# Keys and queries of self-attention moved one group of heads at a time, first maxima between expert sums, and a new order of the stages with warm-up matmuls and early table loads

## The reference, cut to what matters

```python
# layer 0, per sequence
weights = softmax(q @ k.T); evidence = weights @ v
combined = concat([nx, evidence, anchor])
router_probs = softmax(combined @ router_W + router_b)
h = silu(combined @ e_w1 + e_b1); expert_out = h @ e_w2 + e_b2
routed = sum(expert_out * router_probs)
x = x + sigmoid(silu(combined @ gate_w1 + gate_b1) @ gate_w2 + gate_b2) * (routed @ out_w + out_b)
# layer 1, per sequence
h = layernorm(x) * (1 + scale_msa) + shift_msa
x = x + (mha(q, k, v) @ self_o_w + self_o_b) * gate_msa       # self-attention, 512 x 512 scores a head
h = layernorm(x) * norm2_g + norm2_b
x = x + mha(h @ q_w + q_b, context k, context v) @ cross_o_w + cross_o_b
h = layernorm(x) * (1 + scale_mlp) + shift_mlp
x = x + (gelu(h @ mlp_w1 + mlp_b1) @ mlp_w2 + mlp_b2) * gate_mlp
```

## Time and profile before

| | us |
|---|---|
| Median of three runs | 295.75 (294.68 to 296.03) |
| The profiled execution's own time | 295.85 |
| Its span in the profile | 294.1 |
| PE busy | 247.7 (84% of the span) |
| DVE busy | 170.0 (58%) |
| ACT busy | 148.3 (50%) |
| POOL busy | 45.5 (15%) |
| Mean granted clock of TensorE | 0.918 |

### The profile page before, as it was taken

One profiled execution on the slowest core, in us unless ns is written; L12 is line 12 of the kernel. 1 busy time (PEld: TensorE's weight loads), 2 busy tenths in 40 slices (PEclk: granted clock), 3 DMA queues, 4 the chain that ended last, 5 costly groups with the idle time before them and its releaser, 6 DMA issues.

```text
span 294.1 us, 4801 instructions
## 1 busy us (share of the span) xinstructions
PE 247.7 (84%) x1794; PEld 137.3 (47%) x1809; DVE 170.0 (58%) x387; ACT 148.3 (50%) x274; POOL 45.5 (15%) x58
## 2 busy tenths in 40 slices
PE   7699989798288799989999899898898966857686
PEld 2566666358023333344444353444454533545365
DVE  6844418355998987739988756966321652043121
ACT  1215143441017738677667577568778552616352
POOL 1300860247014330001000100010100030001010
PEclk9789999999859999999999999999999995568859
DMA  7989990047410334200210002000003001200001
GB/s 208 400 122 177 149 124 3 0 154 165 129 61 27 112 94 124 82 4 0 76 37 3 6 28 80 4 6 0 2 29 99 2 6 39 68 3 22 0 0 36
DMA packets 15460, 19.72 MB, mean 67 GB/s; under 512 B 3237, under 2 KB 13477, under 8 KB 14445
## 3 DMA queue, kind: packets, MB, share of 16 engines
q1 hardware_dynamic: 15437, 19.42, 26.2%
HBM read 16.19 MB, written 3.03 MB: 65 GB/s over the span
## 4 chain that ended last, share of the span: by engine, by line
PE 43%; ACT 16%; DVE 8%; issue 3%; POOL 0%; ACTq 0%; DVEq 0%; POOLq 0%
PE ps L1147 38%; ACT region L751 10%; DVE neg_max L1025 3%; PE ps L1435 2%; ACT pv_sb L760 1%; DVE neg_max L1034 1%; PE ps L1184 1%; PE ps L1446 1%; ACT L751 1%; DVE normed L850 1%; PE ps L1377 1%; DVE x_sb L1074 1%; ACT nT L654 1%; DVE stats L834 1%; POOL rstd L548 0%
## 5 line engine op out<-in xcount | busy, mean ns | idle before, releaser
L751 ACT ACTIVATE region<-ps 128x512 f32<-128x512 f32 (+1 forms) x160 | 86.6, 594 | 35.2 <-PE ps L1147 33.5
L1025 DVE TENSOR_REDUCE neg_max<-ps 128x2 f32<-128x1024 f32 x64 | 75.5, 1219 | 13.0 <-PE ps L1147 12.7
L1147 PE MATMUL ps<-Qs,k_room 128*128 128x256 bf16 x256 | 43.0, 275 | 3.5 <-ACT region L751 1.4
L1147 PE MATMUL ps<-k_room,Qs 128*128 128x512 bf16 x113 | 35.9, 399 | 8.2 <-DVE neg_max L1025 4.8
L548 POOL TENSOR_TENSOR rstd<-var_eps,minus_half 128x2 f32<-128x2 f32 (+1 forms) x12 | 9.7, 811 | 186.5 <-DVE var_eps L839 186.5
L1147 PE MATMUL ps<-region,V 128*32 128x256 f32 x512 | 37.7, 388 | 1.1 <-ACT pv_sb L760 0.9
L1147 PEld LDWEIGHTS ps<-Qs,k_room 128*128 128x128 bf16 x256 | 19.0, 97 | 31.8 <-ACT region L751 21.5
L1147 PEld LDWEIGHTS ps<-k_room,Qs 128*128 128x128 bf16 x128 | 10.0, 100 | 21.4 <-DVE neg_max L1025 12.8
L1147 PEld LDWEIGHTS ps<-region,V 128*32 128x32 f32 x512 | 12.0, 108 | 15.2 <-issue 9.4
L1063 DVE RECIPROCAL inv_sum<-ps 128x16 f32<-128x16 f32 x16 | 4.1, 254 | 24.4 <-PE ps L1435 24.4
L740 ACT ACTIVATE max_rows<-ps 24x256 bf16<-24x256 bf16 (+2 forms) x13 | 4.8, 370 | 22.3 <-PE ps L1377 22.3
(11 more groups left out here) (159 smaller groups left out, 325.8 us busy)
## 6 DMA issues: line engine op xcount, KB each, us to landing
Qs<-q_scr SPq DMA_DIRECT2D x24, 192.0 KB
k_room<-k_scr SPq DMA_DIRECT2D x4, 576.0 KB
k_room<-in_pad SPq DMA_DIRECT2D x2, 896.0 KB
Qs<-in_pad SPq DMA_DIRECT2D x4, 448.0 KB
q_scr<-q_parts SPq DMA_DIRECT2D x8, 192.0 KB, 2.0
region<-in_w_hidden SPq DMA_DIRECT2D x1, 1344.0 KB, 7.9
w_attn<-in_w_attn SPq DMA_DIRECT2D x1, 896.0 KB, 12.2
k_scr<-k_parts SPq DMA_DIRECT2D x2, 384.0 KB, 2.5
```

The source lines that it names most:

```text
L751: nc.scalar.activation(probs[0:rows_, s % UNITS, j0:j0 + CT // 2, :], ps[0:rows_, EXP0 + e % 2, :].rearrange("p (j n) -> p j n", n=TU), AC ...
L1025: nc.vector.tensor_reduce(neg_max[:, b, t, h:h + MH], ps[:, bank:bank + MH, :], axis=AX, op=ALU.max, negate=True).then_inc(max_read, 1)
L1147: return nc.tensor.matmul(out, lhsT, rhs, start=start, stop=stop)
```

## The change

1. **Stacked by group.** The columns of the q and k weights are ordered by group of heads (`by_group`) instead of by channel over all heads, so that a group's parts are 64 partitions. `send_keys`, `send_queries`, `load_keys` and `load_queries` are each a group at a time, with semaphores of their own; a query load is three transfers of half the size. Cross queries keep their whole-unit path in a scratch tensor of their own (`send_cross`, `load_cross`). High parts of sequence 1 wait for the sends of their own predecessor.
2. **Context keys later.** `send_context` and `load_context` are stages of their own, and stand behind `max:16` and `max:20`. The POOL part (`context_parts`) stands ahead of `expert_bias:1`.
3. **First maxima among expert sums.** `max:0` to `max:3` use banks 0 and 1 alone (FIRST_MAXIMA), so that they can stand between `expert:1.1` and `gated:1`, while the expert outputs hold banks 2 to 5.
4. **New table.** All stages are reordered. New in it are warm runs (`warm:7.5` is five zero products in bank 7 after `max:3`; `warm:2.1`, `warm:0.3`, `warm:0.4` and `warm:4.2` stand near the end), `load_exp:1` ahead of the last cross maxima and `load_gelu:0` behind the last exponentials.

```diff
-hidden:1.6 expert:1.0 context_parts:0 expert:1.1 gate:1 expert:1.2 expert:1.3 gated:1 max:0 max:1 max:2 max:3
...
+expert:1.0 expert:1.1 max:0 gate:1 expert:1.2 load_queries:0.1 max:1 expert:1.3 gated:1 max:2 max:3
...
+        FIRST_MAXIMA = 4
...
         def max_bank(turn):
 
-            return MAX0 + MH * (turn % 2)
+            return MAX0 if turn < FIRST_MAXIMA else MAX0 + MH * (turn % 2)
...
-            def send_keys(b):
-                sp.wait_ge(k_split, b + 1)
-                sp.dma_start(k_scr[b].rearrange("i p n -> p i n"), k_parts[:, :, :]).then_inc(k_out, 16)
...
+            def send_keys(b, g):
+                n = NG * b + g
+                if g == 0:
+                    sp.wait_ge(k_split, b + 1)
+                sp.dma_start(k_scr[n].rearrange("i p n -> p i n"),
+                             k_parts[g * HG * D:(g + 1) * HG * D, :, :]).then_inc(k_out[n], 16)
+
+            def send_queries(u, g):
+                n, b = NG * u + g, u // (NU // B)
+                sp.wait_ge(q_split, Q_SPLITS[("queries", b)] + 1)
+                sp.dma_start(q_scr[n].rearrange("i p n -> p i n"),
+                             q_parts[g * HG * D:(g + 1) * HG * D, :, u % 2 * TU:(u % 2 + 1) * TU]).then_inc(q_out[n], 16)
+
+            def load_keys(b, g):
+
+                n = NG * b + g
+                sp.wait_ge(k_out[n], 16)
+                sp.dma_start(Ks[b][0:MROW, g * HG:(g + 1) * HG, :].rearrange("p h n -> p (h n)"),
+                             k_scr[n].rearrange("j (d h) n -> (j d) (h n)", d=D).unsqueeze(1)
+                             .to_broadcast([NPART * D, NPART, HG * T])).then_inc(k_in[n], 16)
+
+            def load_queries(u, g):
+
+                n = NG * u + g
+                sp.wait_ge(q_out[n], 16)
+                for j in range(NPART):
+                    sp.dma_start(Qs[u][NPART * D * j:NPART * D * (j + 1), g * HG:(g + 1) * HG, :]
+                                 .rearrange("p h n -> p (h n)"),
+                                 q_scr[n].rearrange("i (d h) n -> d i (h n)", d=D)).then_inc(q_in[n], 16)
...
-            def restack_context():
+            def send_context():
                 sp.wait_ge(kc_split, 1)
...
+
+            def load_context():
                 sp.wait_ge(kc_out, 16)
...
+                elif stage == "load_gelu":
+                    nc.scalar.activation(table[:, :], minus_half[:, 0:1], ACT.Gelu_apprx_tanh)
...
-                if first == 0:
-                    pe.wait_ge(q_in[u], 16 * NPART)
                 if first % GROUP_MAX == 0:
+                    pe.wait_ge(q_in[NG * u + first // GROUP_MAX], 16 * NPART)
                     pe.wait_ge(k_in[NG * b + first // GROUP_MAX], 16)
```

More of the change, by code:

```diff
@@ L356, in mixed_expert_attention_kernel @@
         Q_SPLITS = turns("queries", "query")
[L357 to L358 removed]
+        QC_WRITES = {u: i + 1 for i, u in enumerate(x[1] for x in STAGES if x[0] == "query")}
         SPLIT_TURN = turns("max_split")
```

208 lines of the change are left out of this document (101 added, 107 removed).

## The result

The changed kernel takes 290.6 us (median of four runs, 289.64 to 291.64), the kernel before 295.89 beside it: the ratio is 0.985, with an interval of 0.980 to 0.990. By the medians it is 5.3 us faster, by the ratio 4.5, where 5.0 was forecast. The ratios in this document leave out the runs more than 1.5% above the fastest of their kernel, while medians are over all runs. Every batch of runs has its own runs of the kernel before beside it, with medians from 295.64 to 297.04 us, so runs of different batches differ by about 1 us without any edit.

The account below looks back on a forecast made before the run. PE's instruction list was taken to bound 88 to 235 us, DVE the stretch around 70 to 100, a latency chain from 240 on. Terms -2.3 + 2.2 - 5.6 + 0.7 = -5.0 gave 290.8 us, range 285.5 to 296.

Parts of the forecast that it names:

- the middle: Slices 13 to 32, where PE is nearly full: reordering counted as 0, bounds of 3 us either way.
- First softmax: Start of the kernel: sequence 1's scores behind the probabilities' transpose and `route:1` later gain 2.3 us, bounds 0 to 3.
- Maxima among the sums: First maxima between expert sums: PE waits for the load and DVE idles, loss 2.2 us, bounds 0.7 to 4.5.
- The fold: POOL's fold of gates, counted with context keys and cross queries' semaphores: no effect, 0.
- Cross-attention of units 2 and 3: Near the end: earlier scores, query load and exp table bring unit 3's first exponential forward, gain 5.6 us.
- Gelu's table: Table load behind the last exponentials delays the last pv_sb copy: loss 0.7 us, 0 to 0.3 given back.
- Zero products at `max:3`: Five zero products in PE's idle time beside DVE's reductions: value 0.
- The end: Last products at half clock, `warm:4.2` meant for them: taken as 0, bounds 2.8 us gain and 3 loss.
- A: Rival: the table also wins in the middle and at the end by full clock, 286 us; chance 0.2.
- B: Rival, no change: first maxima cost 4.5 us and the query load lands no earlier, 294.6 us; chance 0.18.
- C: Rival, slower: half clock lasts over 5 us past the first exponential, 298 us; chance 0.12.
- D: Rival: warm runs do nothing to the clock at 242, 292.8 us; shares chance 0.5 with the forecast.

Follow-up runs that it names:

- experiment 1: Changed kernel with `fold:1` (four POOL products folding sequence 1's gates) moved back behind `fold:0`; median 290.11 us, ratio 0.978 to the kernel before.
- experiment 2: Changed kernel with the first maxima behind the expert sums again, all four banks in turn; median 291.67 us, ratio 0.984 to the kernel before.
- experiment 3: Changed kernel without the four warm runs near the end, `warm:7.5` kept; median 295.0 us over six runs, ratio 0.984 to the kernel before.
- experiment 4: Changed kernel without `load_gelu:0`, the early load of gelu's table; median 292.49 us over twelve runs, ratio 0.985 to the kernel before.
- experiment 5: Changed kernel with `fold:1` back, first maxima behind the expert sums and no `load_gelu:0`, all together; median 288.71 us, ratio 0.976 to the kernel before.
- experiment 6: Changed kernel with the 512-column product `hidden_x:0.3` ahead of `bias:1`; median 292.43 us, ratio 0.989 to the kernel before.
- experiment 7: Changed kernel with unit 2's cross scores back behind `values_T:cross.2.1`, warm runs kept; one run, 296.03 us, against 295.64 for the kernel before.
- experiment 8: Changed kernel without `load_exp:1`, the early load of exp's table; one run, 296.28 us, against 295.64 for the kernel before.
- experiment 11: Changed kernel without `warm:7.5`, the five zero products behind the first maxima; one run, 293.09 us, against 297.04 for the kernel before.
- experiment 12: Changed kernel once more, nothing changed; one run, 293.71 us, against 297.04 for the kernel before.
- experiment 10: Kernel before with only `scores:1` moved, to behind `scores_T:0`; one run, 298.08 us, against 297.04 for the kernel before.
- experiment 9: Experiment 5's combined version with 13 more zero products at the start; median 285.8 us against 297.04 for the kernel before, ratio of three shortest runs 0.965.

## Why the forecast was right

**The size was right, partly by offset and partly by luck.** -5.0 was forecast and -5.3 measured. Behind the first expert sum -2.7 was forecast (+2.2 - 5.6 + 0.7) and -2.45 measured, in both executions. One loss of 2.6 us was not in that sum, and a gain of 1.4 in the middle, up to the product of unit 3's cross queries, and 1.1 at the end, each inside its bounds but counted as 0, made up for it. Ahead of the first sum -2.3 was forecast. There the two executions have -3.9 and -0.7, with the clock, and the nine profiles of experiments 1 to 8 and 11 begin the sum at 67.60 to 70.57, against 69.08 before. So where the clock falls ahead of the first sum moves the total by as much as the whole term, which the forecast did not count, and experiment 12 beside its own runs of before gives -3.3.

**First softmax: -2.3 forecast, about -1.6 put together from two profiles.** At equal clock the transpose is 1.65 earlier, not 2.3 (experiment 2: 17.94, forecast 17.3). The step that failed in size took the idle time of 0.64 us for a gain on top: the transpose became bound by TensorE's own six products instead of by DVE. From there to the sum it is 49.49 us before and 49.57 after, both at full clock: the 0.78 us of wait that `route:1` takes away (experiment 10 still has it at 42.00) is spent on the scores moved behind. The profile's own 3.9 us contain the clock of one execution, which experiments 1, 10 and 12 show to vary by more than the term itself.

**Maxima among the sums: +2.2 forecast, +1.45 measured.** The mechanism holds in its parts: TensorE waited 2.12 us for the load (2.4 forecast), and DVE idled 0.77 ahead of the second reduction and 1.13 ahead of the fourth (1.25 and 0.7 forecast). Ahead of the first it did not idle at all, where 0.7 was counted: the load took 7.3 us from 59.06 to the first product, where 8.4 were scaled from before. Undone (experiment 2), the maxima give 2.2 us up to the first exponential, 0.8 of it in the wait behind the normalization, which was not among the terms.

**The fold: 0 forecast, +2.6 measured.** This step failed. "Context keys, cross queries' own semaphores, fold of gates ... 0" looked for a wait on POOL and found none. But DVE's four `normed` stood beside POOL's four products, and each lasted as long as the product beside it and a little more: 579 to 1418 ns, median 611, beside 0.46, 0.46, 1.26 and 0.45 us, against 0.28 us alone (1.12 for four). That is 1.87 us, and the wait of 0.77 behind them makes it 2.6. Experiment 1 takes away both; as the wait is missing in experiment 2 too, with the fold still in its new place, it needs the fold and the early maxima together. DVE was the bound of this stretch, as the earlier trace rows said: from the sum to the end experiment 1 needs 219.3 us, 3.2 less than the changed kernel.

**Cross-attention of units 2 and 3: -5.6 forecast, -4.95 measured** from the product of the queries (242.74 to 267.97 before, 241.51 to 261.79 after). By its steps: the send 0.5 nearer to the product (0.6 forecast), 8.47 us from send to cross maxima instead of 10.56 (8.2 forecast), 9.23 to the exponential instead of 11.57 (9.0 forecast). The query load does decide, as far as the trace tells: TensorE stood 2.30 us ahead of 252.56, and the transfers moved 107 GB/s from 250 to 252 and nothing after. Experiments 3 and 7, one profile each, speak for both halves of the step being needed, the order more than the zero products; experiment 8 gives 1.1 to the table load, where 1.28 were counted.

**Gelu's table: +0.7, and nothing given back,** as forecast (experiment 4). The price of a load with a drain did not come: the one-column activation begins at 269.07, 1.29 us after the load's start at 267.78.

**Zero products at `max:3`: 0,** as forecast (experiment 11). **The end: 0 forecast, -1.1 measured,** beside a half clock of 6.8 us instead of 10.2; experiment 9, with none there, has 16.4 us for the stretch, 3.2 less than before, a little past the bound of 2.8.

**The rivals.** A, more gain by a full clock at the end, happened only in experiment 9. B, no change, did not hold: the maxima cost 1.45 and not 4.5, and the query load did come earlier. C, a half clock that outlasts the first exponential, did not occur in any profile; the nearest, of experiment 8, ended at about 95.0, the exponential coming at 96.6. Against D, warm runs without effect, speaks the profile of experiment 3, with its half clock from 240.9 on and 3.0 us more. What is to be kept of the clock rivals is that most of the gain goes together with a higher mean clock. The 39 timed runs of before in the batches of the experiments had mean clocks of 0.908 to 0.941 and spans of 290.2 to 296.3 us; the first four of the changed kernel 0.941 to 0.951 and 287.7 to 289.9. At 0.941, which both reached, before had 290.2 and 291.6, after 289.9. By these three runs the new table is about 1 us ahead at the same clock, too few to build on. And a higher mean clock is in part what the new order brings about, as with the half clock near the end.

**The signs.** Held: TensorE's wait of 2 to 3 us ahead of the first product of k_room and Qs (2.12), no table load between `mlp_down:1` and the exponentials, a middle stretch within 3 us (2.0). Missed: "No half clock from 242 to 256" (it began at 252.9), and the first cross maxima came 2.1 us nearer to their send, not some 3. So by its own words, "or if the clock lies otherwise", the account of the clock near the end was partly wrong. Two readings of the earlier trace rows were loose, and nothing hangs on them: the 14th slice is at 7 tenths, and the clock of the 33rd is 9 tenths.

**Open.** The middle's gain was not taken apart. Nor was it settled why the clock falls in one execution at 18 us and not in another, and so how much of the 2.9 us of the gain that lie ahead of the first sum belongs to the new order. Experiments 7, 8, 10, 11 and 12 are one run each.

## What to carry to other kernels

Where DVE is the bound, look for POOL's work on SBUF (the on-chip memory that both read) beside DVE's, also where neither waits for the other by a semaphore; a fold of weights that is needed late can stand where DVE is not the bound. Zero products of TensorE in gaps that wait for another engine are cheap to try (experiment 9), but one run (experiment 7) says that they do not hold the clock where the order leaves longer waits: shorten the waits by order first, then fill. And compare stretches of two profiles, and whole runs at equal mean clock, before a difference of 1% is given to an edit.

## What the runs showed of the hardware

**DVE and POOL take turns on SBUF.** A view of the four normalizations of the changed kernel (durations in ns, smallest, median, largest):

```profile
L864 DVE TENSOR_SCALAR normed<-x_sb,mean_var,rstd x4: 579/611/1418, 81.4 to 83.7; 128x128 f32<-128x128 f32 x4
```

POOL's durations in the same place are those that it has alone (0.45 to 0.46 and 1.27 us in experiment 1), so only DVE was slowed, by 1.87 us in all. The Trainium skill (SBUF — State Buffer, SBUF: two separate sides) says that the two engines' shared pair of ports is an exclusive lock, held for a whole instruction by whichever starts first, while the other blocks, if the DVE instruction is in a mode with two ports or has two inputs in SBUF while POOL reads there. The trace agrees in the durations: no `normed` is shorter than the POOL product that it stands beside, each ends about 0.08 us after it, and 1418 ns belongs to the one of 1.26 us. It does not show POOL starting first: the four `normed` are stamped at 81.36, 81.86, 82.39 and 83.73, each 0.04 to 0.08 us ahead of its product. Which mode they ran in, no run here shows.

**The clock of one program differs from run to run,** from 0.908 to 0.941 on the mean before the change, with the same instructions. Of the eleven profiles of the changed kernel and its edits without added zero products at the start, eight show half clock between 18 and 30 us, two between 10 and 18, and one none. In experiment 12 TensorE fell to half at 20.0 us, behind a window in which it was busy 4.00 of 4.00 us at full clock. So it was not idle time that came directly before the fall.
